# Set loads of Wv, Wo and W2, and the loads of x, issued from ScalarE's DMA queue instead of SyncE's

## The reference, cut to what matters

```python
h = einsum('bct,bcd->bdt', x, cond_w[subject])      # one 64x64 matrix per sequence
q = layernorm(silu(causal_dwconv4(h @ Wq)));  k = layernorm(silu(causal_dwconv4(h @ Wk)))   # per head, 16 x 128
v = h @ Wv;  beta = sigmoid(h @ Wb + bb);  gate = silu(h @ Wg)
S = (1 - beta) * S + beta * v k^T;  o = S q         # over the 64 tokens, per head
x = x + (o * gate) @ Wo
y = x @ W2^T + adapter(x)                           # adapter of rank 16 per sequence
x = x + quantised_ternary_linear(rmsnorm(y), ffn_w) + bias
```

## Time and profile before

| | |
|---|---|
| median of 3 runs | 2684.84 us (2684.28 to 2686.12) |
| the profiled execution | 2685.08 us, of which the span is 2683.5 us |
| granted TensorE clock, mean over the span | 0.986 |
| TensorE busy | 2556.3 us, 95% |
| VectorE busy | 1688.5 us, 63% |
| ScalarE busy | 1197.7 us, 45% |
| GpSimd busy | 696.3 us, 26% |
| dynamic DMA queue (SyncE's) | 413.63 MB, 48.6% of 16 engines' span |

### The profile page before, as it was taken

How to read it: one execution, slowest core, us unless ns; L and a number is a source line. 1 busy time by engine, 2 the same in 40 slices (tenths; PEclk the granted TensorE clock), 3 DMA queues, 4 the chain that set the end, 5 groups by cost and what they waited for, 6 DMA issues and landing times.

```text
span 2683.5 us, 39968 instructions
## 1 busy us (share of the span) xinstructions
PE 2556.3 (95%) x14536; PEld 1985.0 (74%) x14536; DVE 1688.5 (63%) x2848; ACT 1197.7 (45%) x1878; POOL 696.3 (26%) x764
## 2 busy tenths in 40 slices
PE   5889999999999999999999999999999999999996
PEld 4667777777777777777777777777777777777774
DVE  3766666666666666666656666666666666666653
ACT  3555544544444444354444444353444544444431
POOL 3465522212222212222212222222212212222220
PEclk8999999999999999999999999999999999999998
DMA  6775745445444555355354454444544445444540
GB/s 167 249 224 185 240 154 159 139 155 177 121 142 147 165 166 157 109 172 194 113 173 132 144 177 154 151 139 138 163 148 156 140 149 179 120 146 142 171 132 16
DMA packets 264554, 416.17 MB, mean 155 GB/s; under 512 B 102058, under 2 KB 126634, under 8 KB 264362
## 3 DMA queue, kind: packets, MB, share of 16 engines
q1 hardware_dynamic: 264362, 413.63, 48.6%
HBM read 360.86 MB, written 52.69 MB: 154 GB/s over the span
## 4 chain that ended last, share of the span: by engine, by line
PE 88%; DVE 4%; ACT 3%; issue 2%; SPq 1%; POOL 1%; DMA 0%; ACTq 0%; DVEq 0%; POOLq 0%
PE ring L1048 31%; PE pj_a L1048 26%; PE pj_b L1048 13%; PE ring L1264 4%; PE m L1254 3%; PE var L1222 2%; PE cen_q L1243 2%; PE cen_k L1243 1%; PE cen_k L1244 1%; PE cen_q L1244 1%; PE ring L1149 1%; PE ring L1066 1%; ACT hb L912 1%; PE var L1233 1%; PE m L1264 1%
## 5 line engine op out<-in xcount | busy, mean ns | idle before, releaser
L780 DVE SCALAR_TENSOR_TENSOR y_q<-pj_a,conv,y_q 128x504 f32<-128x504 f32 (+2 forms) x384 | 281.7, 734 | 360.2 <-ACT y_q L963 351.0
L498 POOL TENSOR_TENSOR og_lo<-gt,og_hi 128x512 fp32r<-128x512 f32 x128 | 165.1, 1290 | 922.3 <-ACT og_hi L993 922.3
L1048 PE MATMUL pj_a<-ht_hi,wg 128*128 128x512 f32 x1024 | 352.9, 405 | 2.2 <-DVE y_q L780 2.1
L1048 PE MATMUL pj_a<-ht_hi,wq 128*128 128x512 f32 x1024 | 345.0, 398 | 2.5 <-DVE ht_lo L626 1.5
L1048 PE MATMUL pj_b<-ht_hi,wk 128*128 128x512 f32 x1024 | 335.9, 389 | 0.0
L1048 PE MATMUL ring<-wo,og_hi 128*128 128x512 f32 x1024 | 321.5, 395 | 14.8 <-DVE acc L660 11.8
L1048 PE MATMUL ring<-wv,ht_hi 128*128 128x512 f32 x1024 | 320.8, 394 | 6.8 <-ACT hb L914 6.8
L780 DVE SCALAR_TENSOR_TENSOR y_k<-pj_b,conv,y_k 128x504 f32<-128x504 f32 (+2 forms) x384 | 281.8, 734 | 62.3 <-ACT y_k L963 53.2
L951 ACT ACTIVATE sq_q<-cen_q 128x512 f32<-128x512 f32 x128 | 76.7, 599 | 435.7 <-PE cen_q L1244 435.7
L1048 PEld LDWEIGHTS ring<-wo,og_hi 128*128 128x128 f32 x1024 | 190.4, 189 | 74.2 <-DVE acc L660 18.5
L1048 PEld LDWEIGHTS ring<-wv,ht_hi 128*128 128x128 f32 x1024 | 189.2, 188 | 74.0 <-issue 26.8
(11 more groups left out here) (202 smaller groups left out, 5084.4 us busy)
## 6 DMA issues: line engine op xcount, KB each, us to landing
wq<-parts_q SPq DMA_DIRECT2D x112, 512.0 KB, 4.1
wk<-parts_k SPq DMA_DIRECT2D x112, 512.0 KB, 4.5
wg<-parts_g SPq DMA_DIRECT2D x112, 512.0 KB, 3.7
wv<-parts_v SPq DMA_DIRECT2D x112, 512.0 KB, 6.4
wo<-parts_o SPq DMA_DIRECT2D x112, 512.0 KB, 6.1
keep<-keep_rows SPq DMA_DIRECT2D x256, 64.0 KB, 3.9
wo<-parts_w SPq DMA_DIRECT2D x28, 512.0 KB, 5.6
acc<-in_x_dram SPq DMA_DIRECT2D x8, 1024.0 KB, 5.5
```

Of the source, the lines that this page charges most:

```text
L498: G.tensor_tensor(og_lo[:, u % OG_RING, :], gt[:, u % GT_RING, :], og_hi[:, u % OG_RING, :].bitcast(F32), ALU.subtract).then_inc(S["oglo"], 1)
L780: V.scalar_tensor_tensor(out=yy[:, :, k:], in0=pp[:, :, :L - k], scalar=conv[:, i, h, 3 - k:4 - k], in1=yy[:, :, k:], op0=ALU.mult, op1=AL ...
L1048: last = T.matmul(psum, a, b, start=start and n == 0 and m == 0, stop=stop and n == len(pairs) - 1 and m == 2)
```

## The change

SyncE no longer issues the sets of Wv, Wo and W2, the last W2, and the rows of x for groups 1 to 7. ScalarE issues them, with the same conditions of waiting. The loads of head weights, of the decay rows and of the conditioning matrices and all stores stay in SyncE's queue. On ScalarE a new function `load_sets(U)` stands at the start of each slot, in front of the squares; the first set of Wo of a group (`load_o(g * SETS)`) stands in slot 8 behind `take(U, 0)`; the load of x has moved from the end of slot 12 to the start of slot 13, and the last W2 from slot 127 to slot 128.

```diff
         @block.sync
-            def load_x(g): ...            # the same for load_v, load_o, load_last_w2, load_w2
-            load_x(0)
+            sp.dma_start(acc[:, 0], x_rows[0].rearrange("i p d -> p i d")).then_inc(S["x_in"], 16)
...
             for U in range(SLOTS):
-                if g < GROUPS and h in (0, 4, 8, 12) and g * SETS + h // 4 >= SETS:
-                    for part in range(SET):
-                        load_v(g * SETS + h // 4, part)
-                if h == (1 if g == GROUPS else 2) and g > 1:
-                    for part in range(SET):
-                        load_o(g * SETS - 1, part)
-                if h == 5 and 1 <= g < GROUPS:
-                    for part in range(SET):
-                        load_w2(g - 1, part)
-                if U == UNITS - 1:
-                    for part in range(SET):
-                        load_last_w2(part)
-                if h in (10, 14) and 1 <= g < GROUPS:
-                    for part in range(SET):
-                        load_o(g * SETS + (h - 6) // 4, part)
...
-                if h == 8 and 1 <= g < GROUPS:
-                    for part in range(SET):
-                        load_o(g * SETS, part)
...
                 if h == 12 and g + 1 < GROUPS:
-                    load_x(g + 1)
                     load_cond(g + 1)
...
         @block.scalar
+            def load_x(g):
+                if g == 1:
+                    act.wait_ge(*made("sw", 0, KC - 1))
+                else:
+                    act.wait_ge(S["out_done"], 16 * HT * (g - 1))
+                act.dma_start(acc[:, g % 2], x_rows[g].rearrange("i p d -> p i d")).then_inc(S["x_in"], 16)
...
+            def load_o(s, part):
+                if part == 0:
+                    if s % SETS:
+                        act.wait_ge(*made("o", s - 1, HT - 1))
+                    else:
+                        act.wait_ge(*made("h", s // SETS - 1, HT - 1))
+                n = (s % SETS) * SET + part
+                act.dma_start(block_both("o", n), parts["o"][n]).then_inc(S["wo_in"], 16)
...
+            def load_sets(U):
+
+                g, h = divmod(U, H)
+                for part in range(SET):
+                    if g < GROUPS and h in (0, 4, 8, 12) and g * SETS + h // 4 >= SETS:
+                        load_v(g * SETS + h // 4, part)
+                    if h == (1 if g == GROUPS else 2) and g > 1:
+                        load_o(g * SETS - 1, part)
+                    if h == 5 and 1 <= g < GROUPS:
+                        load_w2(g - 1, part)
+                    if h in (10, 14) and 1 <= g < GROUPS:
+                        load_o(g * SETS + (h - 6) // 4, part)
+                    if U == UNITS:
+                        load_last_w2(part)
+                if h == 13 and g + 1 < GROUPS:
+                    load_x(g + 1)
...
             for U in range(SLOTS):
                 blocks = split_blocks(U) if U < H + 3 else []
+                load_sets(U)
                 if 0 <= U - 1 < UNITS:
                     squares("q", U - 1)
...
                 take(U, 0)
+                if U % H == 8 and H < U < UNITS:
+                    for part in range(SET):
+                        load_o(U // H * SETS, part)
```

More of the change, by code:

```diff
@@ L303, in load_raw @@
                 save_splits(no - SAVE_LAG + 1)
[L305 to L310, removed]
             def load_cond(g):
@@ L993, in gated_hi, with load_v @@
                 A.activation(og_hi[:, u % OG_RING, :], gt[:, u % GT_RING, :], ACT.Identity).then_inc(S["oghi"], 1)
+            def load_x(g):
[4 more added lines that the diff above has]
+                act.dma_start(acc[:, g % 2], x_rows[g].rearrange("i p d -> p i d")).then_inc(S["x_in"], 16)
+            def load_v(s, part):
+                if part == 0:
+                    act.wait_ge(*made("v", s - 1, HT - 1))
+                    if s == SETS:
+                        act.wait_ge(S["saved_v"], 16 * H)
+                n = (s % SETS) * SET + part
+                act.dma_start(block_both("v", n), parts["v"][n]).then_inc(S["wv_in"], 16)
@@ new lines, in load_o, with load_last_w2 @@
+            def load_o(s, part):
+                if part == 0:
+                    if s % SETS:
+                        act.wait_ge(*made("o", s - 1, HT - 1))
+                    else:
+                        act.wait_ge(*made("h", s // SETS - 1, HT - 1))
+                n = (s % SETS) * SET + part
+                act.dma_start(block_both("o", n), parts["o"][n]).then_inc(S["wo_in"], 16)
+            def load_last_w2(part):
+                if part == 0:
+                    act.wait_ge(*made("v", GROUPS * SETS - 1, HT - 1))
+                act.dma_start(block_both("v", part), parts_w2[part]).then_inc(S["wv_in"], 16)
@@ new lines, in load_w2 @@
+            def load_w2(g, part):
+                if part == 0:
+                    act.wait_ge(*made("o", SETS * g + SETS - 1, HT - 1))
+                    if g == 0:
+                        act.wait_ge(S["saved_o"], 16 * H)
+                        act.wait_ge(S["w2_out"], 64)
+                act.dma_start(block_both("o", part), parts_w2[part]).then_inc(S["wo_in"], 16)
+            def load_sets(U):
[13 more added lines that the diff above has]
+                    load_x(g + 1)
```

## The result

The changed kernel took 2713.22 us (median of 4 runs, 2709.91 to 2713.51) against 2684.56 us (4 runs): a ratio of 1.0102, with a 95% interval of 1.0086 to 1.0118. That is 28.7 us slower; +22.8 had been forecast, in a range of 2693 to 2721. The profiled execution took 2713.07 us, its span 2711.3 us, 27.8 us over the span of before.

What follows compares the result with a forecast made beforehand. TensorE, busy 95% of the span, was taken as the bound, with ScalarE lacking slack in slot 8. 12.6 + 10.3 + 0.9 - 1.0 = +22.8 us on 2684.84 gave 2707.6, say 2708 us; 8-in-10 range 2693 to 2721.

Steps and rivals of the forecast that it cites:

- Only TensorE's waits count: TensorE is busy 95% of the span, so moved issues gain or lose only by changing its waits for transfers or chains.
- The slip: Slot 8, groups 1 to 7: issues ahead of silu k lengthen the L1233 wait by 1.8 us each, +12.6 us (4.9 to 22.8).
- a sign of being wrong: Slot 8 on ScalarE: the prediction counts as wrong if the datapath hides more than 0.9 us of the issues.
- The clock: Behind slot 8's longer wait TensorE's clock drops: 2.2 us per group, less 5.1 already paid, +10.3 us (0 to 15.9).
- The last W2: Start of slot 128: issued ahead of the squares, it delays them and TensorE's wait for them, +0.9 us (0 to 1.6).
- Sets at the starts of slots and load_x: Slots 0, 2, 4, 5, 8, 10, 12, 14, and x in 13: squares come late but are absorbed, no cost.
- SyncE's side: SyncE's queue loses waits and issues that TensorE felt once, at a wait for wq: gain 1.0 us (0 to 5.3).
- Two descriptor queues under one lock: Slot 8: ScalarE's and SyncE's issues may wait for each other, 0.3 to 0.6 us per group, left out of the sum.
- Rival 1: Issues hardly hold ScalarE: a set takes 1.6 us, slot 8's chain slips 0.7, no clock change; 2689 us, chance 0.11.
- rival 2: Issues dearer than on SyncE: 3.25 us a set with no overlap, about +39, 2724 us; chance 0.08.
- rival 3: Faster: relieving SyncE's blocked queue removes waits for wq and two without releaser, at most 5.3 us, 2679.5 us; chance 0.03.
- the two unexplained waits: Two TensorE waits without a releaser, 4.3 us together, which might be waits for transfers and so removable.

Runs made afterwards that it cites:

- the run with two and two blocks: Changed kernel with slot 8's set of Wo split, two blocks issued by ScalarE and two by SyncE: 2690.87 us, ratio 1.0022 to the kernel before.
- the run behind r_hi: Changed kernel with slot 8's set of Wo still on ScalarE but after the copy of the row scales: 2686.68 us, ratio 1.0006 to the kernel before.
- The last pair of runs: Silu of k ahead of the last h tile: kernel before, 2668.43 us; changed kernel with Wo set after r_hi, last W2 after the seed, 2668.06 us.
- the three runs with the old wait: Changed kernel with slot 8's set back on SyncE, 2685.43 us; on ScalarE after r_hi, 2686.68; that plus last W2 after the seed, 2684.14.

## Why the prediction was right, and where its sizes were off

- *Only TensorE's waits count; the loss sits in slot 8 behind take(U, 0).* Shown from both sides: the set alone makes +24.5 us, all but it +0.4 us.
- *The slip, forecast 7 x 1.8 = 12.6 us.* Measured 11.3. The set took 2.52 us, like SyncE's 2.51, and 1.0 us of it was hidden (0.9 was estimated, which gives a slip of 1.6, but 1.8 was taken; it was 1.53). The 1.0 us hidden is a little over the 0.9 that the prediction named as a sign of being wrong; the step holds, with that size off by 0.1. The one slow set of group 1 adds 0.6.
- *The clock, forecast +10.3 us.* Measured +12.2. The step that was mis-sized is the interpolation: 2.2 us lost per group were taken between the losses after 3.03 and 5.45 us of idling; seven windows gave 17.2 / 7 = 2.5. After waits of the same 3.39 us the loss was 1.7 in two groups and 2.6 to 2.9 in four; with the set alone on ScalarE it was 2.6 to 2.8 in all seven. The row of 3.03 us itself was one draw of two: the same wait in group 0 lost 1.7 us before and 3.0 in the changed kernel. So this term scatters between groups and between runs, and could not be had more closely from two rows; that the clock read 0.51 to 0.72, and not near 0.65 in all groups, is the same thing. That the idle stretch is its cause is shown by the run with the idle matmuls.
- *The last W2, forecast +0.9.* The wait grew by 0.92 us as reckoned; the clock behind it, 1.6 us more, had been counted for slot 8 and forgotten here.
- *Sets at the starts of slots and load_x, forecast nothing.* Right: 1.0002 with all of them moved, no new wait of TensorE in groups 1 to 7, and the squares 1.0 us late in slot 10, with y_q directly behind the copies and on time.
- *SyncE's side, forecast a gain of 1.0 us.* Wrong: the wait for wq is 0.8 instead of 1.0 us. The step that failed is to take this wait for one that the moved issues cause. In both traces SyncE issues that wq directly behind four stores of parts_o, which were not moved (387.18 to 391.44 us, then wq at 391.49; after the change 388.94 to 393.21, then 393.27); none of the moved loads stands there.
- *Two descriptor queues under one lock, weighed at 0.3 to 0.6 us a group.* In the changed kernel the two queues did not meet in the slot shown: ScalarE's issues ended at 1493.55, SyncE's next one, of wg, began at 1494.06. In the run with two and two blocks, SyncE's pair (1483.52 to 1484.72) and ScalarE's pair (1484.34 to 1485.66) overlap. SyncE's took 1.20 us, ScalarE's 1.32, where the first two issues of a set take 1.20 in the run behind r_hi. ScalarE's first issue, begun while SyncE was still issuing, took its 0.53 us as there. Whatever is shared costs 0.1 us in this slot. By "Perfetto Trace Analysis", section "DMA Instruction — HWDGE (DVE, Sync)" in the Trainium skill, the descriptor generator is locked for one issue at a time, and the wait for the lock is part of the issue's row. By that, ScalarE's first issue should have been longer; it was not, and the measurement decides. "DMA: Bandwidth & Descriptors", section "Issuing engines are not separate DMA queues" in the Trainium skill, says that issuing from several engines saves only the sequencer's time for the issue. The last pair of runs, 2668.4 and 2668.1 us, agrees.
- *Rival 1* (a set holds ScalarE for 1.6 us) and *rival 2* (3.25 us) fall with the 2.52 us in the chain; *rival 3* with the wait for wq and with the two unexplained waits, still 4.3 us together; where the sets cost nothing (ratio 0.9996, and 2668.1 beside 2668.4 us), moving them gains nothing that can be told.
- *The sum.* The terms seen in the trace differ from the forecast by -1.3 (slip), +1.9 (clock), +1.6 (tail) and +1.0 us (SyncE, taken as nothing), so one of them makes up in part for the others. The last 2.7 of the 28.7 us are put down to no term. The upper end of the range, 2721, is nowhere added up in the prediction; 2718 comes out with a slip of 2.5 us and 3.0 us of clock loss in each group.

## What to carry to other kernels

An engine that idles for half of the span can still have no slack in one place, and that place decides what a moved DMA issue costs: follow the chain to each of TensorE's waits before putting anything in front of it. In these runs four issues were free behind 2.5 us of instructions that were ready to run, since the sequencer worked ahead of the datapath; in front of the instruction that others waited for they cost their full length less what was still running, 1.5 of 2.5 us. Expect behind a new wait of TensorE a loss of clock beside its length (here 12 us beside 11, and 14 beside 11 in the run with that set alone), and look first at whether the order around an old wait can be changed: here that was worth 17 us, and the change of queues nothing.

## What the hardware showed that was not expected

- ScalarE's sequencer issued four DMAs while a copy, a table load, the silu and a further copy that stand ahead of them in the program were running or still to run on the datapath: the issues lasted from 1480.20 to 1482.71, the copy began at 1480.46 and the further copy at 1482.91.
- TensorE after 3.39 us of idling lost between 1.7 and 2.9 us to a clock of 1.2 GHz, differing from group to group and from run to run with the same work around it. After 1.85 us it lost 1.7 us in three of seven groups and nothing in four, in this count in each of four traces (the kernel before and the three runs with the old wait), but not in the same groups. With twelve idle matmuls in the gap, and 0.58 us of idling left, the clock behind it was that of 2.4 GHz (1.00) in all seven.
- A set of four issues takes 2.51 us nearly everywhere, and more in single places, on either queue: that of slot 8 in group 1 took 3.25 us on SyncE before, 3.74 on SyncE with the set moved back and 3.11 on ScalarE after, but 2.51 on ScalarE behind r_hi, where another set took 3.37. The cause is open.
